# Linear attention: where VectorE scales the next batch's keys

## The reference, cut to what matters

```python
q = short_conv(hidden_states @ Wq, conv_wq).reshape(b, t, 6, 32)   # four taps, then silu
k = short_conv(hidden_states @ Wk, conv_wk).reshape(b, t, 6, 32)
v = short_conv(hidden_states @ Wv, conv_wv).reshape(b, t, 6, 64)
q = l2norm(q) * dk ** (-0.5)                                       # x * rsqrt(sum(x * x))
k = l2norm(k)
...
S = S * exp(g); pred = k . S; S = S + k (v - pred) beta; o = q . S   # token by token
o = o * rsqrt(mean(o * o) + eps) * norm_weight * silu(gate)
return o.reshape(b, t, 384) @ Wo
```

## Time and profile before

| what | value |
|---|---|
| median of 3 runs | 1369.48 us (1358.34 to 1372.09) |
| profiled execution, its own time | 1379.87 us |
| its span, first to last instruction | 1378.3 us |
| mean granted TensorE clock | 0.903 of full speed |
| busy: PE, DVE, ACT, POOL | 86%, 63%, 45%, 6% |

### The profile page before, as it was taken

The page is one execution under the profiler, slowest core; times in us unless marked ns, Lnnn a source line. Parts: engine busy times, 40 slices in busy tenths (PEclk is TensorE's granted clock), DMA queues, the critical chain, the costliest instruction groups (busy, mean ns, idle before and its releaser), DMA issues. The chain is left out here.

```text
span 1378.3 us, 26691 instructions
## 1 busy us (share of the span) xinstructions
PE 1182.4 (86%) x10170; PEld 994.0 (72%) x10170; DVE 871.2 (63%) x2570; ACT 622.7 (45%) x1591; POOL 81.4 (6%) x90
## 2 busy tenths in 40 slices
PE   4999999899999974999899998358888898868478
PEld 3888789788878863888789887246766677657255
DVE  3767375375737657666656665698787887673423
ACT  4635454353445433434243432447575765534111
POOL 1000000000000001000000001200122111200000
PEclk9999999999999986999999996679798997777689
DMA  8010000000000020000000001100000000000322
GB/s 278 1 62 1 1 1 1 0 0 0 0 1 1 1 85 1 1 1 1 3 1 0 1 1 48 53 26 4 28 28 27 2 29 28 2 1 2 104 69 95
DMA packets 25730, 34.12 MB, mean 25 GB/s; under 512 B 4780, under 2 KB 21004, under 8 KB 25612
## 3 DMA queue, kind: packets, MB, share of 16 engines
q1 hardware_dynamic: 25612, 32.52, 7.3%
HBM read 30.34 MB, written 2.17 MB: 24 GB/s over the span
## 5 line engine op out<-in xcount | busy, mean ns | idle before, releaser
L986 PE MATMUL b_ps<-ln_high,b_high 128*128 128x512 f32 x256 | 101.9, 398 | 26.3 <-PEq L61 20.9
L333 DVE TENSOR_REDUCE a_negmax<-a_ps 128x1 f32<-128x128 f32 x128 | 37.3, 291 | 115.3 <-PE a_ps L514 106.7
L986 PE MATMUL b_ps<-ln_low,b_high 128*128 128x512 f32 x256 | 101.6, 397 | 0.0
L986 PE MATMUL b_ps<-ln_high,b_low 128*128 128x512 f32 x256 | 101.5, 396 | 0.0
L889 DVE TENSOR_TENSOR gate_up_raw<-gate_up_raw,b_ps 128x512 f32<-128x512 f32 x64 | 43.2, 686 | 91.4 <-PE b_ps L986 59.3
L553 PE MATMUL a_ps<-a_wo_high,a_oT 128*128 128x256 f32 x512 | 94.8, 283 | 1.9 <-DVE a_oT L359 1.9
L1013 PE MATMUL b_ps<-b_wd_high,b_mid 128*128 128x256 f32 x512 | 96.4, 283 | 0.0
L945 ACT ACTIVATE gate_up_raw<-b_ps 128x512 f32<-128x512 f32 x64 | 37.5, 599 | 120.6 <-PE b_ps L986 120.5
L477 PE MATMUL a_ps<-ln_high,a_w_high 128*128 128x512 f32 x160 | 69.1, 432 | 14.9 <-PEq L61 14.9
L553 PEld LDWEIGHTS a_ps<-a_wo_high,a_oT 128*128 128x128 f32 x512 | 79.7, 189 | 2.8 <-DVE a_oT L359 2.8
L1013 PEld LDWEIGHTS b_ps<-b_wd_high,b_mid 128*128 128x128 f32 x512 | 80.6, 188 | 0.6
(11 more groups left out here) (376 smaller groups left out, 3061.8 us busy)
## 6 DMA issues: line engine op xcount, KB each, us to landing
d_slots<-in_D_packed SPq DMA_DIRECT2D x16, 433.0 KB, 4.4
c_a_all<-a_scratch SPq DMA_DIRECT2D x8, 768.0 KB, 3.8
x<-in_hidden SPq DMA_DIRECT2D x4, 512.0 KB, 10.1
a_raw<-in_A_q SPq DMA_DIRECT2D x4, 512.0 KB, 7.9
gate_up_raw<-in_A_o SPq DMA_DIRECT2D x1, 2048.0 KB, 13.9
gate_up_raw<-in_B_g SPq DMA_DIRECT2D x1, 2048.0 KB, 12.1
gate_up_raw<-in_B_u SPq DMA_DIRECT2D x1, 2048.0 KB, 8.2
b_wd<-in_B_d SPq DMA_DIRECT2D x1, 2048.0 KB, 10.0
```

Source lines behind the costliest of these rows:

```text
L986: mm = nc.tensor.matmul(ps[:, bank, :], wpart, xpart, start=(j == 0), stop=(j == len(passes) - 1))
```

## The change

VectorE's two multiplications of `keys(c)` move up in VectorE's order. Before, they stand between column 13 and column 14 of the inverse. After, they stand directly behind `mean_square(s, 1)`, ahead of `column_product(m, 11)`. No instruction is added or removed, and no other engine's order changes.

```diff
                     run(c, convolve, 14, 15)
                     run(s, mean_square, 1)
+                    run(c, keys)
                     run(m, column_product, 11)
                     run(c, convolve, 15, 16)
                     run(m, column_sum, 11)
...
                     run(c, convolve, 17, 18)
-                    run(m, columns, 13, 14)
-                    run(c, keys)
-                    run(m, columns, 14, 16)
+                    run(m, columns, 13, 16)
                     run(m, seeds)
```

## The result

The change makes the kernel slower. After it takes 1383.86 us (4 runs, 1383.21 to 1385.10) against 1366.63 us before (4 runs, 1358.34 to 1372.09), a ratio of 1.0132 (95% interval 1.0076 to 1.0189). Measured again later, it was 1387.94 against 1366.57 us, 1.0166 (1.0100 to 1.0231). The profiled execution of after took 1383.21 us, with a span of 1381.6. The forecast was 1359.0.

The account below looks back on a forecast made before the run. With neither PE nor DVE full, waits at the turns between passes were taken to set the time. Five turns' gains, 10.9 us, less 0.4 in one turn gave 10.5, so 1369.5 became 1359.0 us; range 1345 to 1374.

Parts of the forecast that it names:

- a gain of 10.5: Turns between passes: shorter distance from seeds to join_pairs, five turns 9.17 to 7.0 us, one 6.63 to 7.0; 10.5 us.
- POOL and SP: POOL's decayed_keys and gated_outputs and SP's reload start up to 3.5 us earlier; cost 0, within 0.3 us a turn.
- `seeds` stays at 1013.62.: DVE, pass 2 to 3: work from column 14 on keeps its time, as the keys only change place; cost 0.
- the bound of 0.1: DVE: moving the keys costs 0 to 0.1 us a turn, for a covered handover between columns; taken as 0.
- PE idles again, now from 1012.3 to 1014.2, 1.9 us.: PE, pass 2 to 3: after the jobs, pair_part waits 1.9 us for seeds, taking most of PE's saving.
- I take the middle, 7.0.: Seeds to join_pairs in each turn: 7.0 us, between 5.4 and 8.5, the clock behind the new wait being unknown.
- the end of 8.5: Upper limit for seeds to join_pairs, from the last turn's 8.54 us, which has no jobs; gain there 1.2 us.
- rival B: PE's clock falls at the new wait in every turn: distance 8.5, gain 1 us, 1368 us; chance 0.18.
- The other end: Lower limit for seeds to join_pairs, the chain at full clock: 5.4 us; gain 20.1 us if so everywhere.
- The gain belongs to either alike.: The profiled execution, 10.4 us above the median, and the median run both gain the same 10.5 us.
- Rival C: The low clock moves into the joined inverse: net loss 4.8 us per turn struck, kernel slower, 1384 us; chance 0.10.

Follow-up runs that it names:

- hold_gated: The changed kernel with only POOL's two wide multiplications (128x768) held until all 15 columns are summed, decayed_keys staying early; 1375.96 us, ratio to before 1.0082.
- hold_pool: The changed kernel with POOL's decayed_keys, and the work behind them, held until column 13 of the previous batch is summed; 1374.14 us, ratio to before 1.0058.
- fill7: The changed kernel with seven discarded filler matmuls on PE ahead of pair_part, in its wait for seeds; 1361.90 us, ratio to before 0.9959.

## Why the prediction was wrong

The direction was wrong, and the time lies above the range. Two steps failed, and they weigh about the same: a cost of POOL's early work put at 0, and the clock behind the new wait. In the averages of two traces each the first is 9.7 us, and the second made 0.9 of a gain of 10.5. Either alone would have left the time at 1368 to 1369, inside the range; both together put it at about 1378.

*POOL and SP, "I cost them at 0, with 0.3 us a turn to either side for a contended access."* This is the first step that failed. The stretch from the state to `seeds` grew by 18.16 - 16.62 = 1.54 us in a steady turn and by 109.0 - 99.2 = 9.8 us over six; holding POOL back took 1.4 a turn and 8.9 over six of it away in the trace, and 9.7 in the median. The step looked at who waits for what POOL writes, and not at what DVE reads while POOL runs. SP's reload moved too, but it is not the cause: in hold_gated it stayed early and the products were fast, and at after's last turn, where no reload is issued, products 13 and 14 took 1.06 and 1.26 us all the same. The Trainium skill (SBUF — State Buffer, Who interferes with whom) has the rule: a VectorE instruction with both inputs in SBUF and a GpSimd instruction that reads SBUF exclude each other, and the one that came first holds the way for its whole length. The trace agrees, as the three products beside L1679 and L1682 above show. And the trace of before had such a stall already, in its last pass, where no keys are computed; on DVE and on POOL:

```profile
1228.16 2.01 DVE L1754 TENSOR_TENSOR cb_prod<-c_inv,c_urep 128x144 f32<-128x144 f32 x1
```

```profile
1228.10 1.80 POOL L1679 TENSOR_TENSOR cb_o<-cb_o,cb_gate 128x768 f32<-128x768 f32 x1 [33.42 <-ACT cb_o L2054]
```

A product of 0.39 us in the other passes took 2.01, begun 0.06 us behind POOL's. In the steady turns of before, POOL's wide work lay beside `products`, which read PSUM, and beside DVE's wait for the taps; the change took it out of there.

*"`seeds` stays at 1013.62."* It did not, by the step above. The moved keys themselves cost little in their new place: in hold_pool the stretch from the state to `seeds` is 16.78 us a turn for 16.62, so 0.16, a little above the bound of 0.1 that was set. At the old place they covered 0.12 us between the sum of column 13 and the next product (0.24 from the sum to the keys, where it is 0.36 from that sum to the product in hold_pool); at the new one they cover none.

*"PE idles again, now from 1012.3 to 1014.2, 1.9 us."* Right in kind. It was 2.1 us with POOL held and 3.5 in after, the difference being `seeds`.

*"I take the middle, 7.0."* This is the second step that failed. The distance was 8.1 to 8.5 us in all twelve turns of the two traces, near the end of 8.5, so rival B was right for this chain. The loop of the Trainium skill that stood beside it (TensorE: Matmul & The Clock Gate, HAM oscillation) has waits of about 3 to 5 us; here the clock fell behind waits of 2.1 us too, in hold_pool, with distances of 7.2 to 8.5 us. The gain in this term is 52.1 - 50.3 = 1.8 us against the first trace of before and none against the second, instead of 10.5. The other end was right as well: at full clock the chain is 5.42 us, worked out as 5.4. What failed is the choice between the two ends, and the reason given for it, that one wait of 2.57 us had left the clock up: that wait stood ahead of `scores` and the jobs, the new one ahead of `pair_part`. Whether that is the difference was not tried.

*"The gain belongs to either alike."* Wrong in a smaller way. The first trace had 8.6 to 9.4 us in five of six turns; the second had a turn at 6.1 and one at 7.7, so an average execution of before had less to gain than the profiled one.

*Rival C*, slower by the low clock in the joined inverse, named the size and the sign, 1384, but that is luck as far as the runs show. What was to give it away, more than one wait of L1787 above 6 us, is missing: in the first trace of after that wait is 0.6 to 3.2 us in the six turns, and in the second a single one is longer, 7.4. The middle stretch is 109.3 and 114.6 us in after and 113.0 and 104.1 in before: 3.4 us more on average, within what two executions of one kernel differ by. Yet the pattern below the table, 114.4 us with early `scores` against 105.3, speaks for some loss there that came with them; no run isolates it.

Adding up the averages of two traces each, after less before: first `seeds` 3.7, seeds to join_pairs -0.9, join_pairs to state 3.4, state to seeds 9.7; together 15.9, for 17.2 between the medians. The 9.7 is shown by hold_pool and hold_gated. Why the distances gave only 0.9, where 10.5 was forecast, is shown by fill7. Of the 3.7, 0.5 is the change's: in pass 0 product 12 took 0.94 us beside L1672 for 0.43; the rest lies ahead of the first column of pass 0. The 3.4 lies in the stretch that varies by itself. Whether these belong to the change stays open, and so does why hold_pool, with POOL put back and the keys at 0.9 us over six turns, has a median still 7 us above before; its one trace, at 1371.5 us, is level with the mean of the two of before.

## What to carry to other kernels

When a step moves up, list what it releases on the other engines, and for each of those what VectorE will be doing at that time: here POOL's wide multiplications cost VectorE nothing while it waited, read one operand from PSUM or summed a single input, and 0.4 to 1.6 us when it began to multiply two operands from SBUF while POOL's ran. When a wait of TensorE is taken away ahead of a fixed later event, here it came back in front of that event (25.4 us for 28.7); what then counts is which matmuls stand behind it, since in after they ran at the lower clock. A profile of one execution gives durations well and the clock's mixture badly; take two before choosing between ends that hang on it.

## What the runs showed of the hardware that I had not expected

- Two column products of 0.43 and 0.47 us took 1.08 and 1.26 us while POOL multiplied tiles of 128x768, each ending 0.3 us after POOL's instruction.
- Matmuls whose output is thrown away, placed in a wait of 3.5 us, kept the granted clock at 1.00 and shortened the chain behind it by 16 us over six turns, with no useful work changed; the median went from 1383.86 to 1361.90.
- In runs of small matmuls at full clock, PE had gaps of up to 2.33 us with nothing that the profile shows to wait for; in the two traces of after, where the chain behind `seeds` ran at 0.50 to 0.55, there was one, of 0.68 us.
- Executions of one unchanged kernel differed by up to 23 us (1360.14 to 1383.41 for before in one set of 31 runs).
